# Householder tridiagonalisation of a 128x128 matrix inside a fused graph network: the reflector and the update's weights made on ScalarE instead of VectorE

## What is computed

```python
L = jnp.diag(deg) - A
L_norm = d_inv_sqrt[:, None] * L * d_inv_sqrt[None, :]
_, U = jnp.linalg.eigh(L_norm)
agg = jnp.einsum('mn,bnd->bmd', U.T, features)
...
return jnp.einsum('nm,bmd->bnd', U, out)
...
x = _layernorm(x + _L0_gnn_ref(x, adj, ...))   # spectral layer
x = _layernorm(x + _L1_gnn_ref(x, adj, ...))   # two graph convolutions and LSTMs
x = _layernorm(x + _L2_gnn_ref(x, adj, ...))   # attention on the graph
x = _layernorm(x + _L3_gnn_ref(x, ..., adj))   # four-headed attention
```

## Time and profile before

| | |
|---|---|
| median of 3 runs | 1482.2 us (1481.74 to 1482.93) |
| the profiled execution's own time | 1483.62 us |
| span in its profile | 1481.8 us |
| VectorE busy, whole span | 1125.8 us (76%) |
| TensorE busy (matmul), whole span | 1024.0 us (69%) |
| ScalarE busy, whole span | 793.1 us (54%) |
| activation table loads, whole span | 4 of 1.28 us: 1 before the loop, 3 in the layers |
| reflections, from the first L273 (12.85 us) to the last (385.06 us) | 372.2 us, 126 periods of 2.95 us on average |

### The profile page before, as it was taken

One profiled execution on the slowest core, in us unless ns is written; L12 is line 12 of the kernel. 1 busy time (PEld: TensorE's weight loads), 2 busy tenths in 40 slices (PEclk: granted clock), 3 DMA queues, 4 the chain that ended last, 5 costly groups with the idle time before them and its releaser, 6 DMA issues.

```text
span 1481.8 us, 24437 instructions
## 1 busy us (share of the span) xinstructions
PE 1024.0 (69%) x6001; PEld 834.4 (56%) x6001; DVE 1125.8 (76%) x5634; ACT 793.1 (54%) x2905; POOL 172.3 (12%) x464
## 2 busy tenths in 40 slices
PE   5777777777640000008998889988799978899875
PEld 4666666666430000005796666976668956679754
DVE  6888888888799889983457784566865678845677
ACT  3555555555320000004777866777767778677786
POOL 2111111111200000001011010111020120201111
PEclk9999999999975555558999899999899999999987
DMA  0000000000200000001000010000010000100000
GB/s 2 1 1 1 1 1 1 1 1 1 56 20 1 1 1 1 1 0 57 1 2 1 1 39 22 1 1 1 8 53 1 1 1 2 30 0 1 1 1 29
DMA packets 19903, 12.94 MB, mean 9 GB/s; under 512 B 1153, under 2 KB 18722, under 8 KB 19746
## 3 DMA queue, kind: packets, MB, share of 16 engines
q1 hardware_dynamic: 19746, 11.23, 2.8%
HBM read 7.03 MB, written 4.19 MB: 8 GB/s over the span
## 4 chain that ended last, share of the span: by engine, by line
PE 32%; DVE 11%; ACT 8%; issue 2%; POOL 1%; DMA 0%; DVEq 0%; POOLq 0%; ACTq 0%
PE P L1036 11%; PE P L981 6%; PE P L1044 6%; ACT x L1138 2%; PE P L986 2%; ACT S L1209 2%; DVE stats L1248 2%; PE P L1098 1%; DVE S L1320 1%; DVE top L1325 1%; DVE t L1338 1%; PE P L1053 1%; PE P L1082 1%; POOL t L969 1%; ACT t L1189 1%
## 5 line engine op out<-in xcount | busy, mean ns | idle before, releaser
L461 PE MATMUL sumP<-ident_tail,Yb 128*128 128x128 f32 x1 | 0.5, 473 | 215.6 <-DVE Yb L623 215.6
L193 PE MATMUL productP<-M,ident_tail 128*128 128x127 f32 (+63 forms) x254 | 87.3, 441 | 71.3 <-DVE M L313 71.3
L1036 PE MATMUL P<-t,WihT 128*128 128x128 f32 (+1 forms) x832 | 119.4, 290 | 10.9 <-POOL t L969 10.9
L1044 PE MATMUL P<-step_h,WhhT 128*128 128x128 f32 (+2 forms) x768 | 123.4, 304 | 0.0
L490 ACT ACTIVATE small<-small 128x1 f32<-128x1 f32 x1 | 0.2, 203 | 229.1 <-DVE small L596 229.1
L461 PEld LDWEIGHTS sumP<-ident_tail,Yb 128*128 128x128 f32 x1 | 0.2, 183 | 215.7 <-DVE Yb L623 215.7
L1036 PEld LDWEIGHTS P<-t,WihT 128*128 128x128 f32 x832 | 109.9, 191 | 14.4 <-POOL t L969 13.7
L193 PEld LDWEIGHTS productP<-M,ident_tail 128*128 128x128 f32 x254 | 63.6, 311 | 95.1 <-DVE M L313 95.1
L1161 ACT ACTIVATE gate_i<-P,half_bias 128x128 f32<-128x128 f32 (+3 forms) x160 | 69.1, 432 | 89.3 <-PE P L1044 65.3
L962 POOL TENSOR_TENSOR rstd<-variance,minus_half 128x4 f32<-128x4 f32 x64 | 64.5, 1007 | 442.4 <-DVE variance L1258 442.4
L1044 PEld LDWEIGHTS P<-step_h,WhhT 128*128 128x128 f32 x768 | 108.9, 191 | 4.5 <-DVE step_h L1291 0.7
(11 more groups left out here) (322 smaller groups left out, 3159.6 us busy)
## 6 DMA issues: line engine op xcount, KB each, us to landing
xin<-x SPq DMA_DIRECT2D x16, 256.0 KB, 2.8
out<-y SPq DMA_DIRECT2D x16, 256.0 KB, 2.3
W<-L_gnn_W SPq DMA_DIRECT2D x3, 64.0 KB
Wqkv<-L_gnn_W SPq DMA_DIRECT2D x1, 192.0 KB
Wg<-L_gnn_Wg SPq DMA_DIRECT2D x2, 64.0 KB
A<-adj SPq DMA_DIRECT2D x1, 64.0 KB, 2.0
b<-L_gnn_b SPq DMA_DIRECT2D x1, 64.0 KB
bg<-L_gnn_bg SPq DMA_DIRECT2D x1, 64.0 KB
```

Of the source, the lines that this page charges most:

```text
L193: pe.matmul(productP[:, remaining], tails, M[:, remaining], start=True, stop=True).then_inc(product_ready, 1)
L1036: last = pe.matmul(place, c["WihT"][:, p - 1, gate * H:(gate + 1) * H], sources(s, p, t), start=bank not in fresh, stop=not t, skip_group_ ...
L1044: last = pe.matmul(gate_place(s, p, t, gate), c["WhhT"][:, p - 1, gate * H:(gate + 1) * H], step_h[s][:, 0:G * windows(p)], start=False, s ...
```

## The change

The reflector is made on ScalarE (`v_col` is now the column of `reflectors` itself), `BETA` is written straight to `E`'s column and the gain straight to `gains`' column, so the three stores fall away. `E`'s sign is turned once after the loop, on VectorE, and the gains' sign once on GpSimd. The second weight of the update is written as a sum of other products: GpSimd makes `INNER` (reciprocal x `BETA`), VectorE makes `SPREAD` (reciprocal x squared length), ScalarE makes `SPREAD_V`, `GAINED_M`, `INNER_V` and `REST`, and VectorE is left with `PART` and `NU`. `PART` stands ahead of the first half of the update. GpSimd's `INNER` stands ahead of its `open_gain`. After the loop the product for the diagonal is moved ahead of the two operations on `E`.

```diff
 GpSimd, each reflection
                 pool.wait_ge(inverses_ready, now)
                 pool.sem_inc(inverses_seen, 1)
+                pool.wait_ge(beta_ready, now)
+                nc.gpsimd.tensor_tensor(col(INNER), inverses[:, 0:1], E[:, k:k + 1], ALU.mult).then_inc(inner_ready, 1)
                 nc.gpsimd.tensor_tensor(open_gain[:], inverses[:, 1:2], below[:, now:now + 1],
                                         ALU.mult).then_inc(open_gain_ready, 1)
 TensorE
-                reflector = v_col[:, 0:1].to_broadcast([N, N])
+                reflector = reflectors[:, k:k + 1].to_broadcast([N, N])
 ScalarE, each reflection
                 act.wait_ge(beta_ready, now)
+                beta, v_col, gain = E[:, k:k + 1], reflectors[:, k:k + 1], gains[:, k:k + 1]
+                nc.scalar.activation(v_col, ident[:, now:now + 1], ACT.Identity, bias=tail, scale=beta).then_inc(v_ready, 1)
                 act.wait_ge(matrix_ready, now)
-                nc.scalar.activation(col(BETA_M), M[:, now:now + 1], ACT.Copy, scale=col(BETA)).then_inc(beta_m_ready, 1)
-                nc.scalar.activation(E[:, k:k + 1], col(BETA), ACT.Copy, scale=-1.0).then_inc(edges_ready, 1)
+                nc.scalar.activation(col(BETA_M), M[:, now:now + 1], ACT.Copy, scale=beta).then_inc(beta_m_ready, 1)
                 act.wait_ge(v_ready, now)
                 act.wait_ge(gain_ready, now)
-                nc.scalar.activation(col(NGV), v_col[:], ACT.Copy, scale=col(NTAU)).then_inc(scaled_ready, 1)
-                act.wait_ge(scaled_ready, now)
-                nc.scalar.activation(col(NGV_NORM), col(NGV), ACT.Copy, scale=norm).then_inc(scaled_norm_ready, 1)
-                nc.scalar.activation(reflectors[:, k:k + 1], v_col[:], ACT.Copy)
-                nc.scalar.activation(gains[:, k:k + 1], col(NTAU), ACT.Copy, scale=-1.0).then_inc(stored, 1)
+                nc.scalar.activation(col(NGV), v_col, ACT.Copy, scale=gain).then_inc(scaled_ready, 1)
+                act.wait_ge(spread_ready, now)
+                nc.scalar.activation(col(SPREAD_V), v_col, ACT.Copy, scale=col(SPREAD)).then_inc(spread_v_ready, 1)
+                act.wait_ge(beta_m_ready, now)
+                nc.scalar.activation(col(GAINED_M), col(BETA_M), ACT.Copy, scale=gain).then_inc(gained_m_ready, 1)
+                act.wait_ge(spread_v_ready, now)
+                act.wait_ge(inner_ready, now)
+                nc.scalar.activation(col(INNER_V), col(SPREAD_V), ACT.Copy, scale=col(INNER)).then_inc(inner_v_ready, 1)
+                act.wait_ge(gained_m_ready, now)
+                act.wait_ge(coef_ready, now)
+                nc.scalar.activation(col(REST), col(SPREAD_V), ACT.Identity, bias=col(GAINED_M),
+                                     scale=col(COEF)).then_inc(rest_ready, 1)
 VectorE, each reflection
-                V.scalar_tensor_tensor(col(BETA), sign, 1.0, norm, ALU.subtract, ALU.mult).then_inc(beta_ready, 1)
+                V.scalar_tensor_tensor(beta, sign, 1.0, norm, ALU.subtract, ALU.mult).then_inc(beta_ready, 1)
...
-                V.scalar_tensor_tensor(v_col[:], ident[:, now:now + 1], col(BETA), tail, ALU.mult, ALU.add).then_inc(v_ready, 1)
-                whole_row = t.done(V.tensor_tensor(first, first, col(BETA), ALU.add))
+                whole_row = t.done(V.tensor_tensor(first, first, beta, ALU.add))
                 v.wait_ge(inverses_ready, now)
-                V.scalar_tensor_tensor(col(NTAU), inverses[:, 0:1], -1.0, norm, ALU.mult, ALU.mult).then_inc(gain_ready, 1)
+                V.scalar_tensor_tensor(gain, inverses[:, 0:1], -1.0, norm, ALU.mult, ALU.mult).then_inc(gain_ready, 1)
+                V.tensor_tensor(col(SPREAD), inverses[:, 0:1], square, ALU.mult).then_inc(spread_ready, 1)
...
+                v.wait_ge(coef_ready, now)
                 v.wait_ge(open_tail_ready, now)
+                v.wait_ge(v_ready, now)
+                t.wait()
                 V.scalar_tensor_tensor(tail, open_tail[:], col(COEF), col(Q), ALU.mult, ALU.subtract).then_inc(tail_ready, 1)
-                t.done(V.scalar_tensor_tensor(col(NKB), inverses[:, 0:1], -1.0, col(BETA), ALU.mult, ALU.mult))
-                v.wait_ge(gain_ready, now)
-                v.wait_ge(beta_m_ready, now)
-                t.done(V.tensor_scalar(col(NGP), product_colP[:, 0:1], col(BETA_M), col(NTAU), ALU.add, ALU.mult))
+                v.wait_ge(rest_ready, now)
+                part = t.done(V.scalar_tensor_tensor(col(PART), product_colP[:, 0:1], gain, col(REST), ALU.mult, ALU.add))
                 v.wait_ge(p_row_ready, now)
-                t.wait()
-                parts = t.done(V.scalar_tensor_tensor(col(G), p_rowP[:, now:now + 1], col(NKB), col(COEF), ALU.mult,
-                                                      ALU.subtract))
                 v.wait_ge(scaled_ready, now)
                 half = t.done(V.scalar_tensor_tensor(M[:, remaining], p_rowP[:, remaining], col(NGV), M[:, remaining], ...))
-                v.wait_ge(scaled_norm_ready, now)
-                t.until(parts)
-                t.step(V.scalar_tensor_tensor(col(NU), col(NGV_NORM), col(G), col(NGP), ALU.mult, ALU.add))
+                v.wait_ge(inner_v_ready, now)
+                t.until(part)
+                t.step(V.scalar_tensor_tensor(col(NU), p_rowP[:, now:now + 1], col(INNER_V), col(PART), ALU.mult, ALU.add))
 VectorE, after the loop
+            V.tensor_tensor(scrap[:], M[:], ident, ALU.mult).then_inc(diag_ready, 1)
+            t.step(V.scalar_tensor_tensor(E[:, 1:REFLECTIONS], signs[:, 0:REFLECTIONS - 1], 1.0, E[:, 1:REFLECTIONS],
                                           ALU.subtract, ALU.mult))
-            V.tensor_tensor(scrap[:], M[:], ident, ALU.mult).then_inc(diag_ready, 1)
+            t.done(V.tensor_scalar(E[:, 0:REFLECTIONS], E[:, 0:REFLECTIONS], -1.0, None, ALU.mult))
 GpSimd, start of spectral_vectors
-            nc.gpsimd.tensor_tensor(T[:], ident, gains[:], ALU.mult).then_inc(gains_turned, 1)
+            t.step(nc.gpsimd.tensor_tensor(T[:], ident, gains[:], ALU.mult))
+            nc.gpsimd.tensor_scalar(T[:], T[:], -1.0, None, ALU.mult).then_inc(gains_turned, 1)
```

More of the change, by code:

```diff
@@ L103, in spectral_basis @@
     gain_ready = sem("gain_ready")
+    spread_ready = sem("spread_ready")
+    spread_v_ready = sem("spread_v_ready")
+    inner_ready = sem("inner_ready")
+    inner_v_ready = sem("inner_v_ready")
+    coef_ready = sem("coef_ready")
+    gained_m_ready = sem("gained_m_ready")
+    rest_ready = sem("rest_ready")
     beta_m_ready = sem("beta_m_ready")
-    scaled_norm_ready = sem("scaled_norm_ready")
     tail_row_ready = sem("tail_row_ready")
@@ L115, in col @@
         return small[:, j:j + n]
-    (ABS, BETA, NTAU, NKB, COEF, Q, G, BETA_M, NGV, NGV_NORM, NGP, NU, DEGREE, DEG, DI, SOME, EXPONENT, DIAG, ROWSUM,
-     TABLE) = range(20)
+    (ABS, SPREAD, INNER, COEF, Q, BETA_M, GAINED_M, NGV, SPREAD_V, INNER_V, REST, PART, NU, DEGREE, DEG, DI, SOME, EXPONENT,
+     DIAG, ROWSUM, TABLE) = range(21)
     def every_reflection(reflect):
@@ L258, in _ @@
             V.scalar_tensor_tensor(tail, M[:, 0:1], below[:, 0:1], spark[:, 1:2], ALU.mult, ALU.add).then_inc(tail_ready, 1)
-            base_count, per = t.value, 11
+            base_count, per = t.value, 8
             def reflect(k, remaining, parity):
@@ L267, in reflect @@
                 first = row_square[parity][:, now:now + 1]
+                sign, beta, gain = signs[:, k:k + 1], E[:, k:k + 1], gains[:, k:k + 1]
+                norm = divisors[parity][:, 1:2]
                 v.wait_ge(row_copied, now)
-                sign = signs[:, k:k + 1]
-                norm = divisors[parity][:, 1:2]
                 t.done(V.scalar_tensor_tensor(col(ABS), first, -1.0, first, ALU.mult, ALU.max))
@@ L288, in reflect @@
+                V.tensor_tensor(col(SPREAD), inverses[:, 0:1], square, ALU.mult).then_inc(spread_ready, 1)
                 v.wait_ge(product_ready, now)
                 t.until(whole_row)
-                t.done(V.tensor_tensor_reduce(out=scrap[:, remaining], in0=productP[:, remaining], in1=v_row, scale=inverses[:, 0:1], scalar=0.0,
-                                              op0=ALU.mult, op1=ALU.add, accum_out=col(COEF)))
+                V.tensor_tensor_reduce(out=scrap[:, remaining], in0=productP[:, remaining], in1=v_row, scale=inverses[:, 0:1],
+                                       scalar=0.0, op0=ALU.mult, op1=ALU.add, accum_out=col(COEF)).then_inc(coef_ready, 1)
@@ L292, in reflect @@
                 v.wait_ge(product_col_ready, now)
                 v.wait_ge(open_gain_ready, now)
-                t.step(V.scalar_tensor_tensor(col(Q), product_colP[:, 0:1], open_gain[:], spark[:, after:after + 1],
+                t.done(V.scalar_tensor_tensor(col(Q), product_colP[:, 0:1], open_gain[:], spark[:, after:after + 1],
                                               ALU.mult, ALU.subtract))
+                v.wait_ge(coef_ready, now)
                 v.wait_ge(open_tail_ready, now)
```

(24 more changed lines are left out.)

3 lines of the change are left out of this document (removed).

## The result

The changed kernel takes **1504.2 us** (median of 4 runs, 1503.3 to 1505.5) against 1482.6 for the kernel before (median of 4, 1481.7 to 1483.8): ratio 1.0144, interval 1.0129 to 1.0159. It is slower, by 21.6 us; 1515 was forecast, with a range of 1500 to 1530. The profiled execution has a span of 1502.5 us against 1481.8, 20.7 more.

The account below looks back on a forecast made before the run. VectorE's own sequence in the reflection loop was taken as the bound, with ScalarE's chain to `REST` delaying `PART` after the change. +31.8 us (loop) + 0.7 (after it) = +32.5 on the 1482.2 us median: 1515 us, range 1500 to 1530.

Parts of the forecast that it names:

- What bounds the kernel, and the new wait: Reflection loop: VectorE's own sequence of about 2.9 us bounds it; after the change `PART` waits for ScalarE's `REST`.
- ScalarE's chain: Reflection loop: seven ScalarE instructions, 1.73 us from reflector's start to `PART`, 0.25 later on average, +31.8 us in all.
- Waits that are satisfied cost nothing on ScalarE: Reflection loop: already satisfied waits counted at nothing for `NGV`, `INNER_V`, `REST`; 0.07 each would be +27 us.
- The second operand: Reflector and `REST` on ScalarE: a second per-partition operand adds about 0.10 us, giving 0.39 us each.
- rival (a): ScalarE's chain: the second operand costs nothing with one column, chain 1.53 us, +7 us, 1489 us; chance 0.08.
- (b): ScalarE's chain: double waits cost, or an instruction waits for the one before; +27 us, 1542 us; chance 0.06.
- (d): ScalarE: a table load for each change between Sqrt and Identity, +326 us, 1808 us; chance 0.01.
- Row copy's path: Tail to next reflection: row copy comes 0.18 us later but stays hidden, with 0.17 us of cover.
- VectorE idle before `PART`: Reflection loop: VectorE idles some 0.5 us before `PART` in every reflection, about 65 us in all.
- After the loop: Second GpSimd sign instruction, semaphore clearing and moved diagonal product: together +0.7 us; other stages, layers included, unchanged.
- rival (c): Reflection loop: ScalarE's chain ends before VectorE reaches `PART`; -15 us, 1468 us, or nearer 1480; chance 0.05.

Follow-up runs that it names:

- one more in the chain: Changed kernel with an extra ScalarE copy of `SPREAD_V`'s instruction between `SPREAD_V` and `GAINED_M`: 1527.2 us, ratio 1.0303, loop 411.5 us.
- one more behind the chain: Changed kernel with the same extra ScalarE instruction placed behind `REST`: 1502.6 us, ratio 1.0128, loop 389.5 us.
- `open_gain` first: Changed kernel with GpSimd's `open_gain` ahead of `INNER` again: 1502.7 us, ratio 1.0128, loop 388.4 us.
- the rearranged one: Changed kernel with half before `PART`, `open_gain` first, `GAINED_M` on GpSimd, ScalarE reordered, five waits swapped: 1461.8 us; two waits put back: 1457.8 us.
- the reflector alone moved: Kernel before with only the reflector made on ScalarE and its copy dropped, weights as they were: 1482.5 us, ratio 1.0000, loop 367.6 us.
- two pairs swapped the wrong way: Rearranged kernel's swapped waits ahead of the product's reduction and `Q`; putting them back took it from 1461.8 to 1457.8 us.

## Why the prediction was right

- **What bounds the kernel, and the new wait.** Right: `PART` waits for `REST` in 119 reflections and everything of `M`'s update stands behind it. The kernel with one more in the chain and the one with it behind the chain show that this chain sets the period.
- **ScalarE's chain.** The mechanism was right and the size too long: 1.63 us instead of 1.73. It is the term that was mis-sized. I had taken 0.29 us and a distance of 0.20 from an instruction that had waited (L226); in a row without waits they are 0.28 and 0.186. The page of the Trainium skill that I had set against it (ScalarE: Activation LUTs, What ACT_TABLE_LOAD costs) gives, by an estimate from its figures, 1.63 and a sum of 1502 us; the trace of the changed kernel agrees with it, with 279 ns and 1.63 us. I had decided by a row whose instruction was not in the situation of the new ones. With 1.63 the loop's term is (1.63 - 1.48) x 127 = +19 instead of +31.8; measured +17.1, and +18.8 with the late starts of VectorE set aside (4.4 us before, 2.7 after). The chain's error alone is 12.7 us, more than the 9 us that the range allowed for ScalarE's distances; 1504 lies near the range's lower end of 1500, and the slowdown was forecast half as large again as it is. For the same reason the periods became 3.09 us on average and not 3.2.
- **Waits that are satisfied cost nothing on ScalarE.** Right: `NGV`, `INNER_V` and `REST` have two each and follow at 0.18 to 0.19 us.
- **The second operand.** Right: 0.39 us for the reflector, 0.37 for `REST`; so rival (a) falls. ScalarE has no idle time within the chain, so (b) falls with it. So does (d): up to the end of the loop the changed kernel has one table load, before the first reflection, as the kernel before.
- **Row copy's path.** The tail came 0.18 later, as worked out (1.26 behind `BETA` against 1.08), but with a shorter chain the cover was 0.05 and not 0.17. It held: `open_gain` first gave 0.9 us.
- **VectorE idle before `PART`.** Forecast 65 us, measured 38. The forecast's own times give 0.44 us and not 0.5 in a reflection (tail's end at 202.69, `PART` at 203.13), 56 us in all; the chain is 0.10 shorter, which leaves the 0.33 of the 63rd reflection.
- **After the loop.** +1.0 for +0.7. The layers were forecast to be as long as before and took 2.8 us more, at the lower clock that all four executions of the changed kernel show. Whether the change brings that about stays open.
- **Faster, rival (c).** It needed a chain of less than 1.47 us. The change as it was written could not have it; the rearranged one has it, and is faster.

## What to carry to other kernels

Work that goes from the busy engine to an idle one becomes a chain there: add up its distances from the value that starts it to the first instruction that waits for its end, and compare that with the start that this instruction has now, before counting what the busy engine saves. Take the price of an instruction from a row in which it stands as it will stand: the row used here had waited, and that was most of the 0.10 us by which the chain of seven was forecast too long. ScalarE takes 0.19 us for each one-column instruction in a row where VectorE started the next instruction 0.14 us after `PART` (L314 to L317 above), so only results that nobody needs soon belong there. And where an instruction has two waits, write the one that ends last first: here that was worth 20 us in a kernel of 1482, without another edit.

## What the runs showed of the hardware

- The order of two waits ahead of one VectorE instruction: 0.03 to 0.04 us from the end of what it waits for if that wait is written first, 0.10 to 0.11 if second. Three swapped pairs in 127 reflections gave 20.3 us of loop; two pairs swapped the wrong way cost 4.7 (347.9 against 343.2).
- A ScalarE instruction that had to wait lasts 15 ns longer than the same one in a row (294 and 279 ns with one operand, 387 and 372 with two).
- VectorE starts an instruction 0.2 to 0.4 us late at regular places of the unrolled loop (each in every 16th reflection with the reflector alone moved), without a wait that the profile can name. An edit moves these places: 2.7 us in the changed kernel's loop, 4.4 in the one before, 7.9 with the reflector alone moved.
- The layers' time moved between 817.8 and 823.5 us with the granted clock (a mean of 0.94 or 0.93 over stretches at 2.4 and at 1.2 GHz), and with it the whole kernel: the kernel with one more behind the chain gave 1498.6 and 1499.5 us at 0.891 over the whole span, and 1505.7 and 1506.5 at 0.884. A change of 5 us in one stage can be hidden in the total by it, as it was with the reflector moved alone (loop -4.7 us, ratio 1.0000).
